# Separate places for the look-up steps of ScalarE and VectorE, and the group order mix, mix, fold, fold

## The reference

```python
x = x + attention(layernorm(x))      # scores over the feature axis: (512 x 512) for each of 2 batches
x = x + ffn(layernorm(x))
# attention: qT k / sqrt(16) -> softmax over 512 features -> times v -> times Wo
# ffn: h = silu(x @ G.T) * (x @ U.T);  y = h @ D.T
#      G = lut[gate_idx], U = lut[up_idx] (1376 x 512), D = lut[down_idx] (512 x 1376); lut has 16 entries
```

## Time and profile before

| | us |
|---|---|
| median of 3 runs (1107.05 to 1108.62) | 1107.08 |
| the profiled execution | 1108.86 |
| its span, first to last instruction | 1107.04 |
| PE busy in it | 1028.1 |
| DVE busy | 491.6 |
| ACT busy | 467.8 |

### The profile page before, as it was taken

One profiled execution on the slowest core, in us unless ns is written; L12 is line 12 of the kernel. 1 busy time (PEld: TensorE's weight loads), 2 busy tenths in 40 slices (PEclk: granted clock), 3 DMA queues, 4 the chain that ended last, 5 costly groups with the idle time before them and its releaser, 6 DMA issues.

```text
span 1107.0 us, 13011 instructions
## 1 busy us (share of the span) xinstructions
PE 1028.1 (93%) x4744; PEld 844.5 (76%) x4744; DVE 491.6 (44%) x1016; ACT 467.8 (42%) x753; POOL 137.8 (12%) x135
## 2 busy tenths in 40 slices
PE   5888986979889897999999999999999999999997
PEld 4777775767668775788888888888888888888885
DVE  5786867978878987332213122312221222212001
ACT  4987767777867884122122212211221222122110
POOL 4422000000000000002011111111111111111111
PEclk9988998989979999999999999999999999999999
DMA  8853010230101114530022000201020010000000
GB/s 280 266 198 91 8 60 6 84 119 6 46 8 65 60 51 158 207 129 1 1 76 77 1 1 1 78 1 62 15 76 1 1 41 36 1 1 38 1 1 38
DMA packets 31756, 66.04 MB, mean 60 GB/s; under 512 B 3584, under 2 KB 17168, under 8 KB 27088
## 3 DMA queue, kind: packets, MB, share of 16 engines
q1 hardware_dynamic: 26912, 63.06, 15.9%
q10 hardware_dynamic: 4752, 2.16, 0.7%
q0 software_dynamic: 32, 0.01, 0.1%
HBM read 44.18 MB, written 21.04 MB: 59 GB/s over the span
## 4 chain that ended last, share of the span: by engine, by line
PE 66%; DVE 12%; ACT 12%; issue 8%; POOL 1%; DMA 1%; ACTq 0%; POOLq 0%; DVEq 0%
PE bank L1050 34%; PE bank L1058 19%; PE bank L992 8%; ACT part L791 4%; DVE part L1237 3%; PE bank L1093 2%; DVE picked L1237 2%; ACT picked L791 1%; PE bank L1006 1%; PE bank L1039 1%; DVE bn L1214 1%; DVE w_lo L1253 1%; ACT idx_out L872 1%; DVE part L1275 1%; ACT xg_n L882 1%
## 5 line engine op out<-in xcount | busy, mean ns | idle before, releaser
L1050 PE MATMUL bank<-x2t_hi,w_hi 128*128 128x512 f32 (+1 forms) x704 | 278.3, 395 | 22.6 <-ACT h_gate L944 10.3
L1050 PE MATMUL bank<-x2t_hi,w_lo 128*128 128x512 f32 (+1 forms) x704 | 276.8, 393 | 0.0
L1050 PE MATMUL bank<-x2t_lo,w_hi 128*128 128x512 f32 (+1 forms) x704 | 276.6, 393 | 0.0
L1450 DVE TENSOR_TENSOR h_full<-bank,h_gate 128x512 f32<-128x512 f32 (+1 forms) x66 | 45.6, 691 | 396.6 <-PE bank L1050 396.6
L1050 PEld LDWEIGHTS bank<-x2t_hi,w_hi 128*128 128x128 f32 (+1 forms) x704 | 132.1, 188 | 55.6 <-issue 20.6
L791 ACT ACTIVATE part<-high_bit,lut,lut_step 128x512 f32<-128x512 uint8 x198 | 155.4, 809 | 27.3 <-DVE part L1237 24.9
L1050 PEld LDWEIGHTS bank<-x2t_lo,w_hi 128*128 128x128 f32 (+1 forms) x704 | 132.1, 188 | 30.3
L1050 PEld LDWEIGHTS bank<-x2t_hi,w_lo 128*128 128x128 f32 (+1 forms) x704 | 132.4, 188 | 29.5
L740 POOL TENSOR_TENSOR h_lo<-h_full,h_hi 128x512 fp32r<-128x512 f32 (+1 forms) x66 | 85.2, 1291 | 508.1 <-ACT h_hi L968 508.1
L965 ACT ACTIVATE h_gate<-bank 128x512 f32<-128x512 f32 (+1 forms) x66 | 39.4, 598 | 256.3 <-PE bank L1050 256.3
L1058 PE MATMUL bank<-w_hi,h_hi 128*128 128x512 f32 (+1 forms) x324 | 129.6, 400 | 0.1
(11 more groups left out here) (148 smaller groups left out, 1353.3 us busy)
## 6 DMA issues: line engine op xcount, KB each, us to landing
xg<-in_L_attn_x SPq DMA_DIRECT2D x8, 1024.0 KB, 6.3
out_dram<-x1a SPq DMA_DIRECT2D x5, 1024.0 KB, 3.9
x1a<-in_L_attn_x SPq DMA_DIRECT2D x4, 1024.0 KB, 4.8
x1b<-in_L_attn_x SPq DMA_DIRECT2D x3, 1024.0 KB, 4.8
m_hi<-m_scratch SPq DMA_DIRECT2D x3, 1024.0 KB, 5.1
m_lo<-m_scratch SPq DMA_DIRECT2D x3, 1024.0 KB, 7.2
out_dram<-x1b SPq DMA_DIRECT2D x3, 1024.0 KB, 3.9
idx_raw<-in_L_ffn_gate_idx SPq DMA_DIRECT2D x10, 256.0 KB, 6.2
```

Source lines behind the costliest of these rows:

```text
L1050: last = pe.matmul(tile[0:n, :], a, x, start=(k == 0 and j == 0), stop=(k == K - 1 and j == 2))
L1450: dve.tensor_tensor(h_full[0:n, :], bank[5][0:n, :], h_gate[0:n, :], ALU.mult).then_inc(h_done, 1)
```

## The change

The `look` steps and everything that spread them (`look`, `room`, `share`, `leaves_at`, the costs in ns) are gone. Two tables of digits say instead, for each entry of `timeline`, how many look-up pieces ACT and how many DVE does before it; each engine has its own generator. The pieces are finer: on ACT a leaf, the fetch of an index tile and w_hi are one piece each, on DVE every mask. The groups go mix 0, mix 1, fold 0, fold 1, all banks alternate, and T and A of block 0 all stand in fold 1, the fourth A behind its last product. PE's instructions are the same ones, in another order at that place only; the arithmetic is the same.

```diff
-                  (TURN_V, 0), (MIX, 0), (FOLD, 0), (MIX, 1), (FOLD, 1)]
+                  (TURN_V, 0), (MIX, 0), (MIX, 1), (FOLD, 0), (FOLD, 1)]
...
-            return bank[4 * (q % 2 if q < number[(MIX, 1)] else 0) + n % K]
+            return bank[4 * (q % 2) + n % K]
...
-            prepare_pe = {(FOLD, 0): {1: "T0"}, (MIX, 1): {1: "A0 T1", 2: "A1 T2", 3: "A2 T3"}, (FOLD, 1): {0: "A3"}}
+            prepare_pe = {(FOLD, 1): {0: "T0", 1: "A0 T1", 2: "A1 T2", 3: "A2 T3"}}
...
-            look(looks - 1, room(n))
+        prepare(0, "A", T - 1)
         timeline.append(("first", "x2"))
-        early = looked[0]
...
-                share(cost // 2)
-                timeline.append(("silu", item))
+                timeline += [("gate_up", item), ("silu", item)]
...
+        ACT_LOOKS = (
+            "0000000000000000000000000000000000000000000000000000000000000000000000000000000000000001000000000000"
...
+        def with_looks(counts, steps):
+            for k, entry in enumerate(timeline):
+                for _ in range(int(counts[k], 36) if k < len(counts) else 0):
+                    next(steps)
+                yield entry
+            assert next(steps, None) is None
...
+            def look_up():
+
+                yield from make_leaves(0, LEAVES[:LEAVES_AHEAD])
+                for u in range(U):
+                    yield from make_leaves(u, LEAVES[LEAVES_AHEAD:])
+                    if u + 1 < U:
+                        yield from make_leaves(u + 1, LEAVES[:LEAVES_AHEAD])
+                    act.wait_ge(picked_done, u + 1)
+                    if u + 3 < U:
+                        fetch_idx(u + 3)
+                        yield
+                    weight_high(u)
+                    yield
...
-            for stage, arg in timeline:
+            for stage, arg in with_looks(ACT_LOOKS, look_up()):
...
-                    pe.wait_ge(product_lo, K * (number[(MIX, 0)] + 1))
+                    pe.wait_ge(product_lo, K * (number[(FOLD, 0)] + 1))
```

More of the change, by code:

```diff
@@ L280, in tile_of @@
             return picked[u % 2] if j == 0 else part[{1: one, 2: 1, 3: 2, 4: 3, 5: five, 6: one, 7: 2}[j]]
[L282 to L289, removed]
         def make_leaf(eng, u, j):
@@ L305, in preln_attention_ghost_ffn @@
         timeline = []
[L306 to L313, removed]
         def settle(g):
@@ L323, in stats, with normalised @@
             timeline.append(("stats_shift", g))
[L325 to L332, removed]
+        def normalised(n):
+            timeline.extend([("norm", n), ("norm_low", n)])
         idx_per_tile = [(0, 1, 2, 2)[i % 4] if i < T * GB else (i >= T * GB + 4) + (i == T * NG - 1) for i in range(T * NG)]
@@ L371, in preln_attention_ghost_ffn, with prepare @@
                 timeline.append(("mirror", 0))
-            look(LOOKS_GRAM if i >= FIRST_LOOK else 0, 12)
             if 1 <= g < NG - 1 and t == T - 1:
                 timeline.append(("stats_shift", g + 1))
+        def prepare(b, kind, i):
+            if kind == "T":
+                timeline.extend([("turn", (b, i)), ("turn_high", (b, i)), ("turn_low", (b, i))])
+            elif kind == "A":
+                timeline.extend([("attend", (b, i)), ("add", (b, i))])
+                if i == T - 1:
+                    timeline.extend([("stats2", b), ("shift2", b), ("ln2", b)])
+            elif kind == "X":
+                timeline.extend([("x2", (b, i)), ("x2_high", (b, i)), ("x2_low", (b, i))])
         for n in range(K, LAST_ITEM):
@@ L388, in preln_attention_ghost_ffn @@
                 if is_score(n - 1):
-                    normalised(n - 1, room(n))
+                    normalised(n - 1)
                 if not is_score(n + 1):
-                    normalised(n, room(n))
+                    normalised(n)
                 if n < K * (number[(SCORE, 0)] + 1):
@@ L403, in preln_attention_ghost_ffn @@
                 else:
[L404 to L411, removed]
-            look(looks - 1, room(n))
+                    timeline.extend([("turn_high", (0, t)), ("turn_low", (0, t))])
+        prepare(0, "A", T - 1)
         timeline.append(("first", "x2"))
-        early = looked[0]
-        GATE_UP_NS, DOWN_NS, H_NS = 5440, 2720, 1300
-        TURN_NS, ATTEND_NS, EVICT_NS = 400, 2720, 650
         first_plan = ("G0 T0 G1 A0 T1 D0 A1 T2 G2 A2 T3 D1 A3 G3 D2 G4 X0 X1 D3 X2 X3 G5 D4 H0 H1 G6 D5 H2 H3 G7 D6 H4 H5 "
@@ L430, in preln_attention_ghost_ffn @@
         second_plan = ("E10 E0 T0 E1 A0 T1 E2 A1 T2 E3 A2 T3 E4 A3 E5 E6 E7 X0 X1 E8 X2 X3 E9").split()
[L431 to L435, removed]
-        pair_order, second_down_order = [], []
[L437 to L458, removed]
+        pair_order, second_down_order = [], []
         for step in first_plan:
             kind, i = step[0], int(step[1:])
-            cost = free_ns[kind]
             if kind in "GH":
@@ L474, in preln_attention_ghost_ffn @@
                 timeline.append(("down", (0, i)))
-                share(cost)
             else:
-                prepare(1, kind, i, lambda: share(cost))
-        assert looked[0] == OPS * U
+                prepare(1, kind, i)
         timeline += [("y", 0), ("stats1", 2), ("ln1", 2)]
@@ L510, in back_slot @@
             return c if c < 7 else c - 3
-        def built_by(k):
-            return [k // OPS] if k % OPS == OPS - 1 else []
         def scale_of(g):
@@ L922, in _ @@
                     act.copy(lo[:, 1, 0:P], turned[2][:, P:2 * P]).then_inc(mirror_taken, 1)
-                if stage == "look":
-                    make_leaves(arg)
-                if stage == "built":
-                    weight_high(arg)
                 if stage == "first":
@@ L1120, in _ @@
                             pe.wait_ge(idx_laid, U)
-                    pe.wait_ge(product_lo, n - (2 if n // K < number[(MIX, 1)] else 1) * K + 1)
+                    pe.wait_ge(product_lo, n - 2 * K + 1)
                     if name == TURN_V:
@@ L1355, in _ @@
             first = one_block[0]
-            looks = look_up()
-            for stage, arg in timeline:
+            for stage, arg in with_looks(DVE_LOOKS, look_up()):
                 if stage == "lut_step":
@@ L1408, in _ @@
                                              op0=ALU.mult, op1=ALU.subtract).then_inc(product_lo, 1)
-                if stage == "look":
-                    next(looks)
                 if stage == "first":
```

47 lines of the change are left out of this document (27 added, 20 removed).

## The result

| | before | after |
|---|---|---|
| median of 4 runs, us | 1107.85 | 1053.06 (1052.57 to 1053.86) |
| profiled execution, its span | 1108.86, 1107.04 | 1053.47, 1051.70 |
| PE busy | 1028.1 | 1009.0 |
| DVE, ACT busy | 491.6, 467.8 | 490.3, 467.0 |

A forecast was written before the change was run, and what follows sets the result against it. PE was taken to wait for DVE and ACT, themselves partly idle and waiting on each other. Gains of 2 + 0 + 9 + 18 = 29 us gave 1078 us, own range 1068 to 1089, 8-in-10 range 1061 to 1100.

The forecast's parts named there:

- Part 1: Grams and products: look-up pieces moved into ACT's waits for the statistics gain 2 us, between 6 and minus 3.
- If all of those 6.0 went to use, 6: Grams and products: upper case, all 6.0 us of ACT's waits for the statistics are filled and gained; 2 us was taken.
- Part 2: Scores: DVE becomes full with 23 more pieces, 1 us longer but absorbed by PE's own pace: 0, bounds 3 either way.
- Part 3: Mix, fold, attention of block 0: with mix 1 ahead of fold 0, G0 comes at 230.8 instead of 239.95, 9.1 us gained.
- Part 4: Blocks 0 and 1 beside the look-up, from G0 to the last weight: 18 us gained, between 4 and 28.8.
- rival B: PE nearly never waits behind G0 and all else comes too: gain 43 us, 1064 us; chance 0.10.
- The 12.9 us less work for DVE: Behind G0: DVE has 28 fewer look-up pieces left at 0.46 us each, 144.2 us of work instead of 157.1.
- If DVE stayed as loosely packed as now (157.1 of 188.8, 83%): Behind G0: at the old packing DVE's 144.2 us of work take 173.3 us, 15.5 gained.
- The signs: Expected in the changed profile: no hole over 2 us before fold 0, G0 at 227 to 233 us, last w_lo before 410.
- Rival C: Slower: ACT walks its list in order, its 46.3 us of waits grow by 40, giving 1112 us; chance 0.06.
- A: Only the group order gains; behind G0 the separate tables lose packing and eat the earlier start: 13 us, 1094; chance 0.21.
- D: Nothing gained: time won ahead of G0 is waited for at the last w_lo, 1107 us; chance 0.03.

The follow-up runs named there:

- The filler runs: Kernel before plus matmuls that nobody reads in three PE waits (fold 0, G0, second attention tile of block 1): 1106.2 us; with 12 instead of 24 ahead of G0: 1104.2 us.

## Why the prediction was right and wrong

Faster was right, and most of the gain falls where it was forecast; two terms of the sum were far too small, 2 for the grams and 18 for the stretch behind G0, and these are the failed steps.

**Part 1, grams: 2 us forecast, 9.2 measured, 13 to 14 with what follows from it in the scores and mix 0.** The failed step is "If all of those 6.0 went to use, 6": it bounded the gain by one of ACT's waits, and 2 was taken of it. Which instruction is stuck behind a waiting piece, in order, was left out; one such was the take of the Gram matrix, where a w_hi that waited 1.64 us was part of a PE wait that is 2.24 us shorter now. How the 9.2 us divide among such places is not shown. The clock was also lower in this stage (0.87, now 0.96), but with the same places and a clock of 1.00 the stage takes 43.64 us, and with 0.96 it takes 43.69, so the step from 0.96 to 1.00 bought nothing; what 0.87 had cost stays open.

**Part 2, scores: 0 forecast, 1.2 measured, 3.5 with mix 0.** That DVE would be full was right (44.09 of 44.69 us); PE set the pace there, as said. The 3.5 us belong to part 1: they come with the places in the grams and the old ones in the scores too. So 0 for the scores' own places was right. That ACT's leaves there must not follow DVE's table is another matter: tied to it they cost 8.2 us.

**Part 3: 9.1 forecast, 10.5 measured.** The mix 0 to G0 stretch was worked out as 58.5 us and took 57.1; the wait ahead of A3 1.7 and 1.71. But the credit was put in the wrong place: the order of groups alone brought G0 no earlier and gave 2 us in all. With the order alone PE waits for low halves in other places (5.6 us for m_lo); with the tables these waits are gone, and the tables without the order give about half of the 10.5.

**Part 4: 18 forecast, 32.8 measured.** The 12.9 us less work for DVE was nearly right (162.6 to 150.3 us busy, 12.3). The failed step is "If DVE stayed as loosely packed as now (157.1 of 188.8, 83%)", taken as the nearest row. The 18.9 us of DVE's waits were named, and then left inside that packing factor, although the order of instructions showed merges standing in almost each of them; filling them is worth 16 to 19 us, ACT's shorter waits for merges included, which the sum left out. With them gone DVE is busy 89% of the stretch and PE, at 98.5%, is the bound: rival B's case. B's price for this part was 28 us, since it kept G0's slow start (2.8 us) and some 4.5 us of small waits; PE is idle 2.4 us here, and this execution had no slow start at G0. Another of the same kernel had one, and its stretch took 169.3 instead of 168.0 us. Rival B was given 0.10.

**The signs.** As forecast: no hole ahead of fold 0, DVE's waits for the high half under 6 us (3.6), the last w_lo ahead of 410 us (371.4), the rest as long as before. Off: G0 at 216.8 and not 227 to 233: the end of mix 0 came 12.7 us earlier, from the grams, and part 3 gave 1.4 more than forecast. Off too: the idle time ahead of G0, 5.1 + 1.0 us and not 7 to 8. Rival C had its mechanism the wrong way round: ACT's waits of 46.3 us, which it let grow by 40, fell to 10.8. The prediction's own reason, a piece of one engine in the other's way, fits the 32 us that tying ACT to DVE's table cost, for there the waits for ACT's hand-overs grew and not those for merges. A is refuted by the 32.8 us behind G0, D by the 54.8 us.

**The clock.** PE's holes of 9.06, 6.16, 2.21, 3.54 us were followed by half rate; now 5.11 and 1.04 us, with 16 transposes between them, are followed by a first matmul of 0.47 us (full rate) in the one execution, and of 0.77 (half rate) behind 5.09 and 0.91 us in another of the same kernel:

```profile
216.13 0.77 PE L1012 MATMUL bank<-x2t_hi,w_hi 128*128 128x512 f32 x1 [0.91 <-DVE x2t_lo L1293]
```

The Trainium skill ("TensorE: Matmul & The Clock Gate", "HAM oscillation — how this bites in real kernels") says that a kernel pays for the slow start after every hole of enough length. By it, fewer holes should also be a faster clock, and the trace agrees (PE busy 19 us less for the same matmuls). The filler runs show that of 7.8 such us some 3 to 4 were worth time here.

## What to carry to other kernels

- Where two engines hand halves to each other in turn, look for what stands between the two hand-overs in each one's order; independent work belongs there, not behind. 57 small instructions moved so gave 19 us here.
- Price a waiting instruction by what is queued behind it, not by its own wait, and never hide a named wait in a packing factor: take the sum once with it gone.
- Give the background work of each engine places of its own: here ACT's on DVE's places cost 32 us. And a better order on the critical engine gives little while its inputs come late: 2 us here, 8 once they were ready.
- A stage that got shorter need not have done so by its own change. Put the change into one stage alone: the scores' 3.5 us turned out to come from the grams.

## What the runs showed that was not expected

Removed busy time of PE is no measure of the gain: it fell by 19 us at the same instructions, but where fillers alone kept the clock up, only a third to a half of what the half rate had taken was won. In the grams' second half, a clock of 0.96 or 1.00 made no difference to the length of the stage (43.69 and 43.64 us). The same kernel at the same place started G0 at either rate after a hole of 0.9 to 1.0 us, and of the other versions with a hole of 0.91 us there some began at 0.47 us and some at 0.77.
